# A macaron block on one core: first and second job beside each other, last two likewise, probabilities as a ring of 2304 columns

## What is computed

```python
x = x + 0.5 * ffn(layernorm(x))     # dense 256x256 + top-2 of 8 low-rank experts (rank 16)
x = x + attn(layernorm(x))          # latent K/V (rank 64, rms norm, gain g_kv) and Q (rank 128);
                                    # per head 16 content + 32 rotated columns, causal softmax, values of 16
x = x + 0.5 * ffn(layernorm(x))
```

## Time and profile before

| | |
|---|---|
| runs shown | 2213.15, 2213.94, 2213.21 us; median 2213.21 |
| time of the profiled execution | 2213.03 us |
| its span, first to last instruction | 2211.3 us |
| mean granted TensorE clock | 0.969 |
| PE busy | 2043.5 us, 92% |
| DVE busy | 1687.8 us, 76% |
| ACT busy | 1258.5 us, 57% |
| POOL busy | 954.9 us, 43% |

### The profile page before, as it was taken

How to read it: one execution, slowest core, us unless ns; L and a number is a source line. 1 busy time by engine, 2 the same in 40 slices (tenths; PEclk the granted TensorE clock), 3 DMA queues, 4 the chain that set the end, 5 groups by cost and what they waited for, 6 DMA issues and landing times.

```text
span 2211.3 us, 38506 instructions
## 1 busy us (share of the span) xinstructions
PE 2043.5 (92%) x13248; PEld 1570.2 (71%) x13248; DVE 1687.8 (76%) x4926; ACT 1258.5 (57%) x2852; POOL 954.9 (43%) x1566
## 2 busy tenths in 40 slices
PE   3468999999999999999999999999999999999984
PEld 2346777776777777777777777777777777777653
DVE  2448888876887878887888878888788878888841
ACT  3234566665566656665566656656556655556640
POOL 1234454444444444444454544444445444444420
PEclk9669999999999999999999999999999999999996
DMA  2212222122221232122311222222321222221111
GB/s 63 67 44 57 54 79 52 44 66 66 87 52 40 63 87 68 49 68 80 96 40 45 70 71 80 51 70 57 105 54 44 61 79 80 63 64 39 35 30 40
DMA packets 72561, 135.99 MB, mean 61 GB/s; under 512 B 9968, under 2 KB 28656, under 8 KB 72368
## 3 DMA queue, kind: packets, MB, share of 16 engines
q1 hardware_dynamic: 72368, 133.54, 21.9%
HBM read 42.80 MB, written 40.37 MB: 38 GB/s over the span
## 4 chain that ended last, share of the span: by engine, by line
PE 72%; DVE 15%; ACT 5%; issue 3%; DMA 2%; SPq 1%; POOL 1%; POOLq 0%; DVEq 0%; ACTq 0%
PE st_b L561 11%; PE mx_b L590 11%; PE st_b L563 10%; PE o_b L578 9%; PE wj_b L527 5%; PE tp_b L626 4%; PE wp_b L611 4%; PE wp_b L608 3%; DVE xn L820 3%; PE wj_b L516 3%; PE wj_b L502 3%; PE wj_b L528 3%; DVE mx_b L730 3%; DVE st L776 2%; PE wp_b L614 2%
## 5 line engine op out<-in xcount | busy, mean ns | idle before, releaser
L650 ACT ACTIVATE probs<-st_b 128x512 f32<-128x512 f32 (+3 forms) x1536 | 700.0, 491 | 572.1 <-PE st_b L563 406.0
L561 PE MATMUL st_b<-st 113*128 113x512 f32 (+2 forms) x1536 | 576.6, 380 | 9.7 <-DMA st<-shift_scratch 4.5
L730 DVE CUSTOM_DVE_ANT_0 mx_b<-mx_b,tri 128x256 f32<-128x256 f32 (+3 forms) x1024 | 514.2, 513 | 82.5 <-PE mx_b L590 74.5
L590 PE MATMUL mx_b<-st 112*128 112x256 f32 (+2 forms) x1536 | 534.3, 388 | 17.0 <-DVE mx_s L730 11.4
L563 PE MATMUL st_b<-st,k_st 112*128 112x512 f32 (+2 forms) x1536 | 531.3, 351 | 0.0
L926 POOL TENSOR_TENSOR rot_c<-qk,cos_s 128x256 f32<-128x256 f32 x256 | 188.2, 735 | 675.6 <-ACT v_s L660 674.0
L733 DVE TENSOR_REDUCE mx_s<-mx_b 128x1 f32<-128x512 f32 (+1 forms) x512 | 334.0, 652 | 90.9 <-PE mx_b L590 85.9
L776 DVE TENSOR_TENSOR st<-tp_b,st 48x512 fp32r<-48x512 f32 x512 | 352.6, 689 | 38.7 <-ACT st L672 25.8
L590 PEld LDWEIGHTS mx_b<-st 112*128 112x128 f32 x1536 | 276.1, 192 | 125.1 <-issue 46.8
L561 PEld LDWEIGHTS st_b<-st 113*128 113x128 f32 x1536 | 293.0, 191 | 75.4 <-ACT probs L650 25.0
L672 ACT ACTIVATE st<-tp_b 48x512 fp32r<-48x512 f32 x512 | 302.3, 590 | 77.5 <-PE tp_b L626 67.2
(11 more groups left out here) (95 smaller groups left out, 2548.4 us busy)
## 6 DMA issues: line engine op xcount, KB each, us to landing
k_st<-st SPq DMA_DIRECT2D x128, 384.0 KB, 6.0
nx_scratch<-stg SPq DMA_DIRECT2D x16, 768.0 KB, 3.6
cur<-nx_scratch SPq DMA_DIRECT2D x16, 768.0 KB, 4.5
xa<-in_x SPq DMA_DIRECT2D x16, 512.0 KB, 4.6
x_scratch<-xa SPq DMA_DIRECT2D x16, 512.0 KB, 2.7
ao_scratch<-o_f SPq DMA_DIRECT2D x256, 32.0 KB, 1.7
xa<-x_scratch SPq DMA_DIRECT2D x16, 512.0 KB, 3.4
aoc<-ao_scratch SPq DMA_DIRECT2D x16, 512.0 KB, 4.3
```

The source lines that it names most:

```text
L561: nc.tensor.matmul(dst, k1_st[u][0:SHIFT + 1, a, P * j:P * j + P], q_st[u][0:SHIFT + 1, a, q0:q0 + w], start=True, stop=False)
L590: nc.tensor.matmul(mx_b[:, m % 2, 0:w], q_st[u][0:SHIFT, a, P * i:P * i + P], k1_st[u][0:SHIFT, a, k0:k0 + w], start=True, stop=True).then ...
L650: nc.scalar.activation(probs[:, s % PROBS, a, 0:n], st_b[:, a % 2, HALF - n:HALF], ACT.Exp, scale=SCALE).then_inc(exp_done, 1)
L730: nc.vector.tensor_tensor_reduce(src, src, tri[:, HALF - n:HALF], 1.0, NEG, ALU.add, ALU.max, dst).then_inc(mx_done, 1)
```

## The change

**Two lanes.** A second set of the job's tiles is carved out of `probs`, with `o_b` as its bank and semaphores of its own (suffix `_2`). Job 1 and job 31 use it; the other jobs keep the first set. Job 1 is issued beside job 0, job 31 after job 30. Since `probs` and `o_b` belong to the quads in between, the exponentials of quad 0 wait for job 1 (`wj_free_2`, `stored_2`), and job 31's loads wait for the last visit (`pv_done`).

**First latents in place.** Jobs 0 and 1 write `cur` and `kvc` directly; the four transfers through DRAM are gone for the first sequence.

**Start.** The first x is loaded ahead of the weights. The blank rows are written in 8 pieces of 32 x 2048 for each stack: the first stack by ACT among its first steps, the second by POOL (L1019) instead of DVE.

**Probabilities.** `probs` becomes a ring of 2304 columns in which a segment takes only its own width; a visit takes 4, 3, 3 or 2 segments, four visits a quad. An exponential waits for the visit of the last older segment whose place it overwrites (`BEFORE`).

**Transposes.** The stationary side of the transposes is cut to what is used: 112 columns of 128 for `qk`, 72 for the folded maxima, 96 for `kvn`.

**Order.** The tables are new on every engine. The wait of `ao_load` is now for the last W_o product of the job before instead of for all of its matmuls.

```diff
-PROBS = 3
+RING = 2304
...
-PV = [(s, s + 1) for s in range(0, NS, 2)]
+
+PLACE = [sum(ATT[k][3] for k in range(s)) % RING for s in range(NS)]
+BEFORE = []
+for s in range(NS):
+    first, last = PLACE[s], PLACE[s] + ATT[s][3]
+    over = [k for k in range(s - NS, s) if PLACE[k % NS] < last and PLACE[k % NS] + ATT[k % NS][3] > first]
+    BEFORE.append(max(over))
+
+
+PV = [(0, 1, 2, 3), (4, 5, 6), (7, 8, 9), (10, 11)]
 NV = len(PV)
-PV_OF = [s // 2 for s in range(NS)]
+PV_OF = [p for p in range(NV) for _ in PV[p]]
...
+LANE = [0] * NJ
+LANE[1] = LANE[NJ - 1] = 1
+IN_LANE = [sum(LANE[k] == LANE[n] for k in range(n)) for n in range(NJ)]
...
-    return sum(len(job_mm(k)) for k in range(n)) + job_mm(n).index(name)
+    return sum(len(job_mm(k)) for k in range(n) if LANE[k] == LANE[n]) + job_mm(n).index(name)
...
 ORDER = {
     "PE": (
-        "JJJJJJJJJJJJJJPJPJPTPTJTXXJXXTJXXXXJXXJXXJXXJXXFJSSSSSSSSSSSSVJSSPJSSPJPTJPXXTVXXPXXTXXPXXTXXPXXTXXPXXTX"
+        "JJjJjJjjJJjJjjJJJJjjjJjPJPJjPJTJPTPXXTXXXXPXXJTXXJXXTPXJXXTPXXPXXFXXTXXXPXXSTSXSXSXSXPXXTSSXXSSXPXTXSSJX"
...
+BLANKS = 8
...
-        "c": [("load_cur", b, h) for b in range(B) for h in range(2)],
-        "J": jobs([("x_load",), ("x_store",), ("nx_store",)], [("x_load",), ("ao_load",), ("x_store",)]),
+        "c": [("load_cur", b, h) for b in range(1, B) for h in range(2)],
+        "J": [(name, n) for n in range(NJ) if LANE[n] == 0 for name in SP_STEPS[JOBS[n][0]]
+              if name != "nx_store" or n > 1],
+        "j": [(name, n) for n in range(NJ) if LANE[n] == 1 for name in SP_STEPS[JOBS[n][0]]
+              if name != "nx_store" or n > 1],
...
-        probs = sb("probs", [P, PROBS, HQ, HALF])
+        probs = sb("probs", [P, HQ, RING])
...
+        room = probs[:, :, :].rearrange("p a c -> p (a c)")
...
+        lanes = [Lane(sb, sb, wj_b, ""), Lane(carve(0), carve(GT * HALF * 2), o_b, "_2")]
...
+        def latents(n):
+
+            if n > 1:
+                return stg[:, :, :], kvs[:, :, :]
+            return cur[:, HT * n:HT * n + HT, :], kvc[0:KR, HT * n:HT * n + HT, :]
+
+        def blank(u, k):
+
+            row, value = (ODD - 32, 0.0) if k < 6 else (P - 32, 1.0)
+            flat = k2_st[u].rearrange("p a t -> p (a t)") if k in (4, 5) else st[u].rearrange("p s a t -> p (s a t)")
+            c = 2 * T * (k - 4 if k >= 4 else k)
+            return row, flat[row:row + 32, c:c + 2 * T], value
...
+            def load_first():
+                sp.dma_start(hb_s[:, :], bias.rearrange("(a n) -> a n", a=1).to_broadcast([P, D])).then_inc(hb_in, 16)
+                sp.dma_start(w1_s[:, :, :], w1.rearrange("(k p) n -> p k n", p=P)).then_inc(w_in, 16)
+                sp.dma_start(bt_s[:, :], bt).then_inc(w_in, 16)
...
+                    if done and LANE[n]:
+                        sp.wait_ge(pv_done, NV * QUADS)
+                    sp.dma_start(own.xa[:, :, :], x_g[k] if kind == JOB_A else x1_d[k]).then_inc(own.x_in, 16)
                     if n == 0:
+                        load_first()
+                    elif n == 1:
...
+                    if LANE[n]:
+                        sp.wait_ge(pv_done, NV * QUADS)
+                    else:
+                        earlier = [i for i in range(n) if LANE[i] == LANE[n] and JOBS[i][0] == JOB_C]
+                        if earlier:
+                            sp.wait_ge(own.wj_full, bank_use(earlier[-1], "wo1") + 1)
...
-                        last = nc.tensor.transpose(wj[:, P * tk:P * tk + P],
-                                                   kvn[:, tk:tk + 2, :].rearrange("p t n -> p (t n)"), ident[:, :])
-                last.then_inc(wj_full, 1)
+                        last = nc.tensor.transpose(wj[0:TWO, P * tk:P * tk + P], flat[:, KR * tk:KR * tk + TWO],
+                                                   ident[:, :])
...
+                    on_diag = [k for k in PV[p] if ATT[k][4]]
+                    if on_diag:
+                        pe.wait_ge(masked, len(DIAG) * g + DIAG.index(on_diag[-1]) + 1)
+                    if not ATT[s][4]:
                         pe.wait_ge(exp_done, UNITS * g + HQ * (s + 1))
...
-                                                    v_s[q][:, j, a, :], probs[:, s % PROBS, a, 0:n],
+                                                    v_s[q][:, j, a, :], probs[:, a, PLACE[s]:PLACE[s] + n],
...
-                    nc.tensor.transpose(tp_b[:, 0, 0:P], mxf[h2][:, :], ident[:, :]).then_inc(tp_full, 1)
+                    nc.tensor.transpose(tp_b[0:FOLD, 0, 0:P], mxf[h2][:, 0:FOLD], ident[:, :]).then_inc(tp_full, 1)
...
-                        pe.wait_ge(cur_in[k // HT], 32 * (g // NQ + 1))
+                        if g:
+                            pe.wait_ge(cur_in[k // HT], 32 * (g // NQ))
+                        else:
+                            pe.wait_ge(lanes[k // HT].wj_free, bank_use(k // HT, "kvt") + 1)
...
-                        last = nc.tensor.transpose(tp_b[:, 0, P * c:P * c + P], flat[:, P * c:P * c + P], ident[:, :])
+                        last = nc.tensor.transpose(tp_b[0:TURN, 0, P * c:P * c + P], flat[:, P * c:P * c + TURN], ident[:, :])
...
-            for stack, row, factor in ((st[0].rearrange("p s a t -> p (s a t)"), ODD - 32, 0.0),
-                                       (k2_st[0].rearrange("p a t -> p (a t)"), ODD - 32, 0.0),
-                                       (st[0].rearrange("p s a t -> p (s a t)")[:, HQ * T:], P - 32, 1.0)):
-                rows = stack[row:row + 32]
-                last = nc.scalar.activation(rows, ones[row:row + 32, 0:1].to_broadcast(rows.shape), ACT.Copy, scale=factor)
-            last.then_inc(blanked, 1)
...
-                    if a == 0 and NS * g + s >= PROBS:
-                        old_g, old_s = divmod(NS * g + s - PROBS, NS)
-                        act.wait_ge(pv_done, NV * old_g + PV_OF[old_s] + 1)
-                    nc.scalar.activation(probs[:, s % PROBS, a, 0:n], st_b[:, a % 2, HALF - n:HALF], ACT.Exp,
+                    if a == 0:
+                        old_g, old_s = divmod(NS * g + BEFORE[s], NS)
+                        if old_g >= 0:
+                            act.wait_ge(pv_done, NV * old_g + PV_OF[old_s] + 1)
+                        elif s == 0:
+                            act.wait_ge(lanes[1].wj_free, len(job_mm(1)))
+                            act.wait_ge(lanes[1].stored, 16)
+                    nc.scalar.activation(probs[:, a, PLACE[s]:PLACE[s] + n], st_b[:, a % 2, HALF - n:HALF], ACT.Exp,
...
-                    elif g == 1 and k == 1:
-                        nc.vector.memset(f32(st[1])[ODD - 32:ODD, :, :, :], 0.0)
-                        nc.vector.memset(f32(k2_st[1])[ODD - 32:ODD, :, :], 0.0)
-                        nc.vector.memset(f32(st[1])[P - 32:P, 1, :, :], 1.0).then_inc(blanked, 1)
...
+                elif name == "blank":
+                    _, rows, value = blank(1, arg[0])
+                    nc.gpsimd.memset(rows.bitcast(F32), value).then_inc(blanked[1], 1)
+                    pool.wait_ge(blanked[1], arg[0] + 1)
```

More of the change, by code:

```diff
@@ L1 @@
+import math
 from contextlib import ExitStack
@@ L191, in quads, with lane_jobs @@
     return [(name, g, *arg) for g in range(QUADS) for name, *arg in steps]
-def jobs(before, after):
-    return [(name, n, *arg) for n in range(NJ) for name, *arg in (before if JOBS[n][0] == JOB_A else after)]
+def lane_jobs(lane, before, after):
+    return [(name, n, *arg) for n in range(NJ) if LANE[n] == lane
+            for name, *arg in (before if JOBS[n][0] == JOB_A else after)]
 PROJ = quads(*[("proj", k) for k in range(TB)])
@@ L207 @@
 FFN_POOL = [("aggr", 0)] + [("bias", k) for k in range(GT)] + [("gated",)]
+SP_STEPS = {JOB_A: ("x_load", "x_store", "nx_store"), JOB_C: ("x_load", "ao_load", "x_store")}
+BLANKS = 8
 STREAMS = {
@@ L215 @@
         "F": quads(("mx_turn", 0), ("mx_turn", 1)),
-        "J": [("job", n, name) for n in range(NJ) for name in job_mm(n)],
+        "J": [("job", n, name) for n in range(NJ) if LANE[n] == 0 for name in job_mm(n)],
+        "j": [("job", n, name) for n in range(NJ) if LANE[n] == 1 for name in job_mm(n)],
     },
@@ L221 @@
         "H": HALVES,
-        "J": jobs(FFN_ACT + LAT_ACT, FFN_ACT),
+        "J": lane_jobs(0, FFN_ACT + LAT_ACT, FFN_ACT),
+        "j": lane_jobs(1, FFN_ACT + LAT_ACT, FFN_ACT),
+        "B": [("blank", 0, k) for k in range(BLANKS)],
     },
@@ L234 @@
         "K": quads(*[("mask", s) for s in DIAG]),
-        "J": jobs(FFN_POOL + [("aggr", 1), ("ss",)], FFN_POOL),
+        "J": lane_jobs(0, FFN_POOL + [("aggr", 1), ("ss",)], FFN_POOL),
+        "j": lane_jobs(1, FFN_POOL + [("aggr", 1), ("ss",)], FFN_POOL),
+        "B": [("blank", 1, k) for k in range(BLANKS)],
     },
@@ L497, in job @@
                     if k == 0:
-                        pe.wait_ge(ao_in, 16 * (JOBS[n][1] + 1))
+                        pe.wait_ge(own.ao_in, 16 * (sum(JOBS[i][0] == JOB_C and LANE[i] == LANE[n] for i in range(n)) + 1))
                     for tt in range(2):
```

(11 more changed lines are left out.)

578 lines of the change are left out of this document (299 added, 279 removed).

## The result

The changed kernel takes 2155.23 us, median of 4 runs (2151.76 to 2156.78); the kernel before, on the same chip, 2213.57 (2213.15 to 2217.41). The ratio is 0.9731, with a 95% interval of 0.9714 to 0.9747: 58 us less, 2.7%, where 2124 (89 us less) was forecast and the range ended at 2154.

A forecast was written before the change was run, and what follows sets the result against it. PE, busy 92% of the span, was taken as the bound, its loss lying at the two ends. 2213.0 - 60 (start) - 21 (visits) - 8.4 (end) = 2123.6, forecast 2124 us; own range 2108 to 2140, 8-in-10 range 2096 to 2154.

The forecast's parts named there:

- the pace of 0.1518: Steady part: PE's time an instruction, forecast to fall from 0.1538 to 0.1518 us with four visits a quad.
- 1. The start: Jobs 0 and 1 side by side, latents in place: -60 us, bounds -39 and -76.
- Rival A: Start gives only 28 to 45 us, as POOL's memsets set job 0's start: 2139 to 2156; chance 0.18.
- 2. The visits: Steady part: two visits fewer in each of 32 quads, 0.33 us each, booked in full: -21 us.
- The lower bound of 8 us for the term: Visits: at least 8 us gained if two thirds come back as waits of the new order.
- 4. At nothing: Narrower transposes, the ring, the remaining aoc waits (12.4 us stay): booked at no gain or loss.
- 3. The end: Job 31 starts at 2163.1 instead of 2171.6, its loads ahead of job 30's store: -8.4 us, bounds -5 and -10.
- the ring: Probabilities: 2304 columns, largest visit 1536, 768 left for ACT, whose slack covers it; booked at nothing.
- B: Visits do not pay: long visits starve DVE, PE waits behind each, the 21 us go: 2145; chance 0.14.
- C: Slower: PE waits for DVE's maxima or masks; 2.8 us a quad loses the whole gain, 3.2 gives 2226; chance 0.05.

The follow-up runs named there:

- the first run: Changed kernel with only SyncE's order mended: x and aoc loads issued ahead of the k_st copies, two places a sequence; 2111.98 us, ratio 0.9532.
- the full-width run: Changed kernel with all transposes at the full 128 output partitions again, nothing else moved; 2156.03 us, ratio 0.9729.
- the six visits: Changed kernel with six value visits of two segments a quad instead of four longer ones, PE's order moved to fit; 2233.64 us, ratio 1.0082.
- the run of the jobs in turn: The first run's kernel with jobs 0 and 1 in turn on four engines at the start instead of interleaved; 2154.01 us, ratio 0.9742.
- both orders mended: Changed kernel with SyncE's loads ahead of the k_st copies and VectorE's statistics behind three more maxima and two evacuations; 2123.15 us, ratio 0.9573.

## Why the prediction was wrong, by its own steps

**The sum's terms against the traces:** start forecast -60, measured -67.4; visits and all else of the middle forecast -21, measured +10.5 (-16.0 from quad 1 to quad 8, of which 13.9 once, +26.5 from there to the last score); end forecast -8.4, measured -4.4. Together -61.3 in the traces. A sum also hid a slip: the pace of 0.1518 took all 21 us off a stretch that holds some 25 of the 32 quads; by the same 0.33 it should have been 0.1522.

**1. The start: right.** The first evacuation was put at 26 and came at 24.70; the first projection at 71.5, came at 68.30; POOL's pieces of 2048 columns took 1.80 us each (forecast 1.8 to 2.1). The rows in the timeline of the start:

```profile
5.42 7.39 POOL L1019 MEMSET st<- 32x2048 f32 x4 [1.27 <-DVE kvc L807]
...
24.70 0.60 ACT L794 ACTIVATE xt<-wj_b 128x512 f32<-128x512 f32 x1 [9.80 <-PE wj_b L586]
...
68.30 0.55 PE L693 MATMUL wp_b<-wq_s,cur 128*128 128x192 f32 x2
```

Rival A is out. That POOL's pieces delay job 0 was right as well; moving them won 7 us at the first score, of which half was given back.

**2. The visits: the failed step.** "This is PE's own time and PE is the bound there, so I book it in full." The price was right (0.32 measured by itself), and in the four quads from 1 to 5, where nothing is late, the kernel gains 2.1 of the 2.6 us that eight visits fewer should give. But the step took the rest of the steady part as unchanged, and the sentence under 4 on `aoc` says so outright: "the other 12.4 stay, since `ao_load` still stands behind `x_load`". I looked at what stands between the two loads and at PE's distance, and not at what else stands ahead of both on SyncE's queue: the copies of `k_st`, at two places a sequence. This cost 44 us by the first run. The lower bound of 8 us for the term did not hold either, since it allowed waits to eat two thirds of the gain, and not more than the gain; the clock behind them was in no bound. With SyncE's order mended, the whole kernel stands at 2112 in a range of 2108 to 2140. That it comes out 12 us below the 2124 is in part luck: against the kernel before, the trace of that run gives 32.5 us in the middle (21 forecast), because a single wait of 5.18 us for `aoc`, which the prediction left in place, is gone too; the start gives 65.3 (60 forecast) and the end 4.9 (8.4 forecast).

**3. The end: mechanism right, size half.** Job 31's first product follows job 30's last with no wait, as forecast (2111.39). But `aoc` was there about 5.7 us earlier (issued at 2101.36, plus 4.3): job 30 itself was late, and PE stood 5.28 us for its routing, a wait of 0.26 before:

```profile
2100.59 1.09 PE L598 MATMUL wj_b<-ident,xn 128*128 128x128 f32 x4 [5.28 <-POOL xn L1039]
```

Two things in the new orders lead there. PE's last product that the routing needs starts 1.1 us ahead of the last visit (2093.34, 2094.46), where it was 4.4 (2146.97, 2151.38), so less work covers the routing; and DVE has quad 31's output steps between its pieces, which now take 4.3 us where they took 3.1. Neither was moved by itself. Putting job 31's first product ahead of job 30's second output step won 2.6 us.

**4. At nothing: right for the transposes** (the full-width run) and for the ring, though its room is not free of waits: ACT waits for a visit 4 times, 10.8 us in total, where it waited 85 times, 151.8 us, before. PE's waits for ACT's probabilities are 4.3 us in total, so nothing of size came of either. It was wrong for `aoc`, as told.

**The rivals.** B's number (2145) is the nearest to the result, and its mechanism was not the cause: with the long visits kept and two loads moved, the waits and 44 us are gone, and cutting a long visit in two costs 0.32 us instead of giving time back. The waits of PE for `mx_b` did grow, as it said (from 14.4 us in total to 21.1), but at the place where they are long DVE stood for a DMA and not for want of banks of maxima. C's mechanism appeared in the six visits, in my own order.

## What to carry to other kernels

When a change rewrites an order, read for each load that a wait hangs on everything that now stands ahead of it on its queue, not only its neighbour, and compare the distance to its first reader; two copies ahead of two loads here became 44 us. A stall can have two prices, its own length and what the clock does with it, so a term that may leave PE waiting 2 us deserves a bound with the half clock in it. A price per piece of work (0.33 us a visit) can be right and the term still wrong, because the term also claims that the rest stays as it was.

## What the runs showed of the hardware that I had not expected

- In the steady part PE's waits of 1.44 and 1.45 us left the granted clock at 1.00; with those of 2.22, 3.21 and 8.12 us came 3.4, 6.8 and 10.2 us at 0.50, and with one of 5.18 us in the kernel before 6.8. The half clock can begin inside the wait: at 995.0 in the one of 8.12 us, which ends at 1000.14. The wait's length does not decide alone: in the changed kernel 1.95 us (from 648.5) was followed by 3.4 us at 0.50, while 1.96 us in the run of the jobs in turn (from 273.8) was not; and of two waits of 1.07 us for `probs`, the one with both orders mended (from 2031.2) had 3.4 us at 0.50 with it, the one in the first run (from 2019.4) none. How much of a wait's cost is clock was worked out from the length of these stretches, and not tried apart from the wait.
- The load of a transpose's stationary side takes 135 ns at 112 columns and 142 at 128, while the transposes they belong to take 275 ns each way.
- The time of an issue on SyncE's queue differed for one and the same transfer with what stood ahead: the first copy of `k_st` takes 1.28 us behind the latents' store and 0.63 behind `aoc` in the first run, and `aoc` 2.21 behind the copies and 0.41 ahead of them. Why was not tried.
